# A mixture-of-experts stage that fetches its token tiles by lists: one-hot products in place of scattered rows, three routing groups, W2 split by GpSimd

## The reference, cut to what matters

```python
logits = einsum('bsd,de->bse', x, router_W) + router_b     # x: after a layernorm
probs = softmax(logits); top1 = argmax(probs)              # 8 experts, one for each token
h = relu(einsum('bsd,edf->besf', x, W1) + b1)              # 256 -> 1024
y = einsum('besf,efd->besd', h, W2) + b2                   # 1024 -> 256
out = x_before_norm + one_hot(top1) * probs . y            # only the chosen expert counts
```

## Time and profile before

| | us |
|---|---|
| median of 3 timed runs (lowest, highest) | 2818.48 (2810.91, 2821.3) |
| the profiled execution | 2812.32 |
| its span, first to last instruction | 2810.5 |
| busy: PE, DVE | 2571.2, 1928.8 |
| busy: ACT, GpSimd | 1322.4, 1132.5 |
| the mixture in the span | from 2441.6 |

### The profile page before, as it was taken

The page is one execution under the profiler, slowest core; times in us unless marked ns, Lnnn a source line. Parts: engine busy times, 40 slices in busy tenths (PEclk is TensorE's granted clock), DMA queues, the critical chain, the costliest instruction groups (busy, mean ns, idle before and its releaser), DMA issues. The chain is left out here.

```text
span 2810.5 us, 50716 instructions
## 1 busy us (share of the span) xinstructions
PE 2571.2 (91%) x16973; PEld 1551.5 (55%) x16989; DVE 1928.8 (69%) x3654; ACT 1322.4 (47%) x2007; POOL 1132.5 (40%) x853
## 2 busy tenths in 40 slices
PE   7997899999967899999999999999889999749998
PEld 4775333333335556565656565656444444448997
DVE  5776798998778765657575756566477776665555
ACT  2433477666668643434343434333245554443333
POOL 3323433333047253535453535444454443152333
PEclk9999799999979999999999999999989999859999
DMA  5001322222111000000000000000133332246665
GB/s 171 0 0 40 78 66 62 64 72 59 32 60 46 1 2 2 1 1 1 2 1 1 1 2 1 2 1 1 52 83 86 77 84 71 55 155 229 218 214 194
DMA packets 105254, 160.71 MB, mean 57 GB/s; under 512 B 30877, under 2 KB 65704, under 8 KB 99432
## 3 DMA queue, kind: packets, MB, share of 16 engines
q1 hardware_dynamic: 100056, 148.01, 18.4%
q0 software_dynamic: 3408, 8.46, 0.8%
q10 hardware_dynamic: 1600, 1.61, 0.2%
HBM read 91.66 MB, written 14.96 MB: 38 GB/s over the span
## 5 line engine op out<-in xcount | busy, mean ns | idle before, releaser
L1647 ACT ACTIVATE self_PT<-self_ST 128x1024 f32<-128x1024 f32 x256 | 263.0, 1027 | 483.1 <-PE self_ST L1586 480.5
L1667 DVE TENSOR_REDUCE self_nmax<-self_SM 128x2 fp32r<-128x1024 f32 x256 | 313.1, 1223 | 199.1 <-PE self_SM L1569 198.5
L1735 POOL TENSOR_TENSOR self_U<-self_PT 128x1024 f32<-128x1024 f32 x64 | 153.1, 2392 | 498.5 <-ACT self_PT L1647 498.5
L496 DVE TENSOR_REDUCE cross_nmax<-cross_S 128x2 f32<-128x1024 f32 x256 | 307.5, 1219 | 47.0 <-PE cross_S L350 44.9
L1738 POOL TENSOR_TENSOR self_U<-self_U,self_PT 128x1024 f32<-128x1024 f32 x128 | 303.9, 2374 | 82.2 <-ACT self_PT L1647 80.0
L441 ACT ACTIVATE cross_PT<-cross_S 128x1024 f32<-128x1024 f32 x256 | 259.9, 1025 | 124.4 <-PE cross_S L361 124.0
L1596 PE MATMUL self_W<-self_PT,self_V 128*64 128x512 f32 x1024 | 233.8, 598 | 0.0
L1141 DVE TENSOR_REDUCE cross_nmax<-cross_S 128x4 f32<-128x1024 f32 x128 | 156.5, 1223 | 92.7 <-PE cross_S L968 91.6
L1078 ACT ACTIVATE cross_PT<-cross_S 128x1024 f32<-128x1024 f32 x128 | 131.1, 1024 | 128.0 <-PE cross_S L984 127.7
L1596 PEld LDWEIGHTS self_W<-self_PT,self_V 128*64 128x64 f32 x1024 | 67.8, 136 | 131.8 <-issue 115.6
L1569 PE MATMUL self_SM<-self_k_hi,self_q_hi 64*128 64x512 f32 x512 | 117.7, 456 | 22.9 <-DVE self_nmax L1667 20.1
(11 more groups left out here) (450 smaller groups left out, 6893.6 us busy)
## 6 DMA issues: line engine op xcount, KB each, us to landing
moe_staged<-in_L_ffn_W SPq DMA_DIRECT2D x36, 1024.0 KB
cross_ks<-cross_parts SPq DMA_DIRECT2D x384, 64.0 KB, 2.3
cross_qs<-cross_parts SPq DMA_DIRECT2D x376, 64.0 KB, 2.3
all_x<-in_L_ffn_W SPq DMA_DIRECT2D x14, 1024.0 KB
all_x<-sorted_rows SPq DMA_DIRECT2D x83, 130.0 KB, 2.2
cross_cT<-in_ctx_T SPq DMA_DIRECT2D x16, 512.0 KB, 4.6
sorted_rows<-all_spare_row SPq DMA_DIRECT2D x1, 5460.0 KB, 23.8
all_x<-in_x SPq DMA_DIRECT2D x8, 512.0 KB, 9.2
```

The costliest lines, as they stand in the source:

```text
L496: dve.tensor_reduce(nmax[:, g % 2, 0:R, n % PER_G], S[:, slot[st], :, :], AX.X, ALU.max, negate=True).then_inc(s_maxed, 1)
L1647: act.activation(PT[:, k, :, :], ST[:, :, :], ACT.Exp).then_inc(exped.sem, 1)
L1667: dve.tensor_reduce(nmax[:, i:2 * NT:NT], SM[:, :, :], AX.X, ALU.max, negate=True).then_inc(maxed.sem, 1)
L1735: pool.tensor_tensor(U[:, c % 2, :, :], PT[:, 0, :, :], PT[:, 1, :, :], ALU.add).then_inc(added.sem, 1)
```

## The change

Rows are no longer sorted in memory. x, with 1/std and -mean/std, is written as it stands to DRAM (`rows_mem`, 4097 rows of 258 words, the last one zeros), by four DMAs that ACT issues ahead of the normalisations of a stretch. For each routing group, now three of 12, 12 and 8 tiles, DVE splits each token's position into a tile and a lane (`spread`), and forms two one-hot arrays: lanes (tokens x 128) and slots (tokens x 42, once times the token's number less 4096, once times its gate). PE multiplies them (`invert`) and adds up over all tiles in one PSUM bank, so that column n holds the list of slot n: for each lane the token's number and its gate. DVE adds 4096 and copies the lists (`places`, `gates`); an empty lane gets number 4096, the row of zeros, and its output is dropped.

The product of a group stands in PE's order ahead of the logits of pair 11 (group 0), behind the last logits (group 1) and behind the last count (group 2). GpSimd gathers each slot's tile from `rows_mem` by an indirect DMA, two slots further ahead than SP did, and `rest` is a copy that ACT makes of xs (`keep`). In the loop SP is left with W1 alone. Experts 0 to 6 get their low part of W2 from GpSimd, behind its roots and ahead of the gathers; expert 7's is DVE's, behind the lists. ACT makes the high parts two pieces at a time at pairs 3 to 6, 9 to 12 and 15 (`PIECES`), 18 of 32, and the other 14 after the last exponentials. W1 of slot 0 waits for the owners and for the four writes of x. The filling of the 5.46 MB at the start is one row now.

```diff
-XROW = C + 4
-GATE, TOKEN, RSTD, SHIFT = C, C + 1, C + 2, C + 3
-GROUPS, NORMS = ((0, 4), (4, 12), (12, 22), (22, 32)), ((0, 4), (4, 12), (12, 22), (22, 32))
-
-
-SPLIT_FROM = 3
+XROW = C + 2
+RSTD, SHIFT = C, C + 1
+SPARE = B * T
+GROUPS, NORMS = ((0, 12), (12, 24), (24, 32)), ((0, 4), (4, 12), (12, 22), (22, 32))
+
+
+PIECES = (0, 0, 0, 2, 2, 2, 2, 0, 0, 2, 2, 2, 2, 0, 0, 2)
+LOWS_BY_DVE = (7,)
...
+    hot_lanes, hot_tiles = (m.hid_hi, m.hid_lo), s.sb("hot_tiles", [P, MOST, 2, N_SLOTS])
...
+    def low_part(eng, e):
+        eng.wait_ge(s_w2_hi, FF // 2 * (e + 1))
+        eng.tensor_tensor(m.W2[:, e, :, 1, :], m.staged[:, e % 2, :, :], m.W2[:, e, :, 0, :].bitcast(F32),
+                          ALU.subtract).then_inc(m.s_w2_low[e % 2], 1)
...
-                sp.wait_ge(m.s_w2_low, e - 1)
+                sp.wait_ge(m.s_w2_low[e % 2], e // 2)
             sp.dma_start(m.staged[:, e % 2, :, :], a["L1_ffn_W2"][e].rearrange("(k p) n -> p k n", p=P)).then_inc(s_w2[e % 2], 16)
-        sp.wait_ge(s_sc, 16 * NX)
...
-        def scatter(g):
-            first, last = GROUPS[g]
-            pool.wait_ge(s_pos, g + 1)
-            for t in range(first, last):
-                pool.indirect_dma_start(out=sorted_rows, out_offset=bass.IndirectOffsetOnAxis(ap=position[:, t:t + 1], axis=0),
-                                        in_=x_rows[:, t, :], in_offset=None).then_inc(s_sc, 16)
...
-        for g in range(G):
-            scatter(g)
+        for e in range(E):
+            if e not in LOWS_BY_DVE:
+                low_part(pool, e)
...
+        def spread(g):
+            first, last = GROUPS[g]
+            n = last - first
+
+            def per_slot(v):
+                return v[:, 0:n].unsqueeze(2).to_broadcast([P, n, N_SLOTS])
+
+            step(dve.tensor_scalar(tile_of[:, 0:n], row[:, 0:n], P / 2 - 0.5, 1.0 / P, ALU.subtract, ALU.mult))
+            step(dve.tensor_scalar(tile_of[:, 0:n], tile_of[:, 0:n], ROUND, None, ALU.add))
+            step(dve.tensor_scalar(tile_of[:, 0:n], tile_of[:, 0:n], ROUND, None, ALU.subtract))
+            step(dve.scalar_tensor_tensor(out=lane_of[:, 0:n], in0=tile_of[:, 0:n], scalar=-float(P), in1=row[:, 0:n], op0=ALU.mult, op1=ALU.add))
+            if g:
+                dve.wait_ge(s_inv, g)
+            for at, to in ((0, min(n, FF)), (FF, n)):
+                if at < to:
+                    step(dve.tensor_tensor(hot_lanes[at // FF][:, 0:to - at, :], lane.unsqueeze(1).to_broadcast([P, to - at, P]),
+                                           lane_of[:, at:to].unsqueeze(2).to_broadcast([P, to - at, P]), ALU.is_equal))
+            placed, gated = hot_tiles[:, 0:n, 0, :], hot_tiles[:, 0:n, 1, :]
+            step(dve.tensor_tensor(placed, slot_no.unsqueeze(1).to_broadcast([P, n, N_SLOTS]), per_slot(tile_of), ALU.is_equal))
+            step(dve.tensor_tensor(gated, placed, per_slot(gate), ALU.mult))
+            step(dve.tensor_tensor(placed, placed, token[:, first:last].unsqueeze(2).to_broadcast([P, n, N_SLOTS]), ALU.mult))
+            dve.sem_inc(s_spread, 1)
...
             place(g)
-            if g < G - 1:
-                low_parts(g)
+            spread(g)
...
+        dve.wait_ge(s_inv, G)
+        step(dve.tensor_scalar(taken[:, :], inverse[:, 0, :], float(SPARE), None, ALU.add))
+        step(dve.tensor_copy(m.places[:, :], taken[:, :]))
+        step(dve.tensor_copy(m.gates[:, :], inverse[:, 1, :]))
+        dve.sem_inc(m.s_places, 1)
+        for e in LOWS_BY_DVE:
+            low_part(dve, e)
...
+        def invert(g):
+            first, last = GROUPS[g]
+            pe.wait_ge(s_spread, g + 1)
+            for t in range(first, last):
+                of = lanes_of(t - first)
+                done = pe.matmul(INV[:, 0:2 * N_SLOTS], of.bitcast(F32), hot_tiles[:, t - first, :, :].rearrange("p v n -> p (v n)"),
+                                 start=(t == 0), stop=(t == NX - 1), skip_group_check=True)
+            done.then_inc(s_inv, 1)
...
-            if 2 * m - 2 in [first for first, _ in GROUPS[1:]]:
+            if 2 * m - 2 in firsts:
                 count_of(group_of(2 * m - 2) - 1)
+            if 2 * m - 10 in firsts:
+                invert(group_of(2 * m - 10) - 1)
             logits(m)
+        invert(G - 2)
         count_of(G - 1)
+        invert(G - 1)
...
+                        act.dma_start(rows_mem[first * P:last * P, :].rearrange("(n p) c -> p n c", p=P), x_rows[:, first:last, :]).then_inc(s_rows, 16)
...
-            if i >= SPLIT_FROM:
-                high_part(i - SPLIT_FROM)
+            for piece in range(sum(PIECES[0:i]), sum(PIECES[0:i + 1])):
+                high_part(piece)
...
+    def keep(act, j):
+        act.copy(rest[:, j, :], xs[:, j, 0:C]).then_inc(s_kept, 1)
+
+    def gather(pool, n):
+        pool.indirect_dma_start(out=xs[:, n % DEEP, :], out_offset=None, in_=consts["rows_mem"],
+                                in_offset=bass.IndirectOffsetOnAxis(ap=m.places[:, n:n + 1], axis=0)).then_inc(s_loaded[n % DEEP], 16)
...
+        sp.wait_ge(m.s_rows, 16 * len(NORMS))
         m.load_w1(sp, 0, expert_of(sp, 0))
+        sp.dma_start(b2B[:, :], a["L1_ffn_b2"].rearrange("e c -> (e c)").unsqueeze(0).partition_broadcast(P)).then_inc(s_b2, 16)
...
-                following, stored = sp.snap(t * DEEP + (j + DEEP)), sp.snap(t * DEEP + (j + DEEP - 1))
-                sp.wait_ge(s_normed, t * DEEP + (j + 1))
-                sp.dma_start(xs[:, j, :], tiles[bass.ds(following, 1), :, :].rearrange("a p c -> (a p) c")).then_inc(s_loaded[j], 16)
                 sp.wait_ge(s_first, t * DEEP + (j + 1))
                 m.load_w1(sp, j, expert_of(sp, t * DEEP + (j + DEEP)))
-                k = (j + DEEP - 1) % DEEP
-                sp.wait_ge(s_freed, t * DEEP + (j + DEEP))
-                sp.dma_start(rest[:, k, :], tiles[bass.ds(stored, 1), :, :].rearrange("a p c -> (a p) c")).then_inc(s_rest[k], 16)
...
                 high_by_act(act)
+                act.wait_ge(s_y, t * DEEP + (j + 1))
+                keep(act, (j + 2) % DEEP)
...
-                dve.wait_ge(s_rest[j], t * 16 + 16)
+                dve.wait_ge(s_kept, t * DEEP + (j + 1))
                 dve.wait_ge(s_freed, t * DEEP + (j + 1))
-                dve.scalar_tensor_tensor(out=y[:, j, :], in0=z[:, :], scalar=rest[:, j, GATE:GATE + 1], in1=rest[:, j, 0:C],
+                dve.scalar_tensor_tensor(out=y[:, j, :], in0=z[:, :], scalar=m.gates[:, bass.ds(t * DEEP + j, 1)], in1=rest[:, j, :],
...
+        pool.wait_ge(consts["filled"], 16)
+        pool.wait_ge(m.s_rows, 16 * len(NORMS))
+        pool.wait_ge(m.s_places, 1)
+        for n in range(DEEP):
+            gather(pool, n)
         pool.wait_ge(s_hi_act, 1)
         low_by_pool(pool)
+        for n in range(DEEP, DEEP + 2):
+            pool.wait_ge(s_kept, n - DEEP + 1)
+            gather(pool, n)
         for n in range(SLOTS):
             pool.wait_ge(s_hi_act, n + 2)
             low_by_pool(pool)
+            if n + DEEP + 2 < SLOTS + AHEAD:
+                pool.wait_ge(s_kept, n + DEEP)
+                gather(pool, n + DEEP + 2)
             pool.wait_ge(s_y, n + 2)
...
         def fill(sp):
-            sp.wait_ge(s_id2, 2)
-            sp.wait_ge(s_spare, 16)
-            sp.dma_start(sorted_rows.rearrange("(g p) c -> p g c", p=P),
-                         spare_row[:, :].unsqueeze(1).to_broadcast([P, SLOTS + AHEAD, XROW])).then_inc(s_filled, 16)
+            sp.wait_ge(s_id2, 1)
+            sp.dma_start(rows_mem[SPARE:SPARE + 1, :], spare_row[:, :]).then_inc(s_filled, 16)
```

More of the change, by code:

```diff
@@ L2665 @@
 AHEAD, DEEP = 3, 3
-XROW = C + 4
-GATE, TOKEN, RSTD, SHIFT = C, C + 1, C + 2, C + 3
-GROUPS, NORMS = ((0, 4), (4, 12), (12, 22), (22, 32)), ((0, 4), (4, 12), (12, 22), (22, 32))
-SPLIT_FROM = 3
+XROW = C + 2
[4 more added lines that the diff above has]
+LOWS_BY_DVE = (7,)
 class MoeBuffers:
     def __init__(self, s, x_all, a):
-        self.s_w2_low, self.s_owned, self.s_b1 = s.sem("w2_low"), s.sem("owned"), s.sem("b1_in")
+        self.s_w2_low, self.s_owned, self.s_b1 = [s.sem(f"w2_low{n}") for n in range(2)], s.sem("owned"), s.sem("b1_in")
+        self.s_places, self.s_rows = s.sem("places"), s.sem("rows")
         self.s_w1 = [s.sem(f"w1_in{n}") for n in range(DEEP)]
@@ L2773, in route, with lanes_of @@
     s_w2, s_w2_hi = [s.sem(f"w2_in{n}") for n in range(2)], s.sem("w2_hi")
-    s_d, s_less, s_exp, s_hot, s_cnt, s_pos, s_sc = (s.sem(n) for n in ("d", "less", "exp", "hot", "cnt", "pos", "sc"))
+    s_d, s_less, s_exp, s_hot, s_cnt, s_pos = (s.sem(n) for n in ("d", "less", "exp", "hot", "cnt", "pos"))
+    s_spread, s_inv, s_rows = s.sem("spread"), s.sem("inv"), m.s_rows
+    def low_part(eng, e):
+        eng.wait_ge(s_w2_hi, FF // 2 * (e + 1))
+        eng.tensor_tensor(m.W2[:, e, :, 1, :], m.staged[:, e % 2, :, :], m.W2[:, e, :, 0, :].bitcast(F32),
+                          ALU.subtract).then_inc(m.s_w2_low[e % 2], 1)
+    def lanes_of(t):
```

(22 more changed lines are left out.)

70 lines of the change are left out of this document (28 added, 42 removed).

## The result

The changed kernel takes 2831.7 us (median of 5 runs, 2828.33 to 2833.5), against 2813.21 for the kernel before in the same comparison (5 runs, 2810.91 to 2821.3): a ratio of 1.0053, 95% interval 1.0036 to 1.007. By the ratio it is slower by about 15 us (the two medians are 18.5 us apart), just beyond the 0.5% that was set as the edge of no change; the interval reaches to both sides of that edge. The forecast was 2825, with 2803 to 2838 around it and most of the chance (0.65) within 0.5%. The profiled execution took 2830.98 us, its span is 2829.2.

What follows compares the result with a forecast made beforehand. PE bounds the loop, and a chain through 32 scatters the routing's end. Routing +10.5 and start -1.0 sum to +9.5 on the profiled 2812.32, so 2821.8; 2825 us was forecast for the measured median, range 2803 to 2838.

Steps and rivals of the forecast that it cites:

- The holds: In routing, GpSimd's low parts block DVE's steps with two SBUF operands: 4.7, 9.1 and about 9.5 us on the path.
- The owners: End of routing on DVE: the owners' table, 2.9 us of work with three groups, ready at 2538.3.
- the lists: End of routing: slot lists there at 2539.7, after 3.4 us for invert 2 from 2535.5.
- Invert 0: PE's product for group 0, ahead of pair 11 and so on the path: 5.2 us for 12 tiles.
- a low part: GpSimd's 128x2048 subtraction for an expert's W2 in routing: 4.55 us, bounds 4.3 and 5.0.
- The first rival: In routing, low parts run beside DVE or fall into its waits for PE: 2804 us; chance 0.20.
- The first gather: Between lists and first product: 2.9 us from issue to landing, then 1.7 for norm, turn and copy.
- The start: PE's first projection, behind a barrier after the filling, begins at 17.0 through the one-row filling: -1.0 us, or 0.
- The loop: The 39 slots, with fewer SP DMAs and an added gather and copy: cost 0, bounds 0 and +0.3 a slot.
- the second rival: The loop leaves PE because the gather delays DVE's last step: 39 x 0.3 = 12 us, together 2837; chance 0.15.
- the choice of +10.5: Delay of the first product taken as 2542.9, between sums of 2544.4 (12.0 late) and 2541.
- The third rival: In routing, half of the holds fall into waits: first product 2532 to 2538, time 2815 to 2819; chance 0.15.

Runs made afterwards that it cites:

- e2: The changed kernel with GpSimd filling the low parts of experts 0 to 6 with zeros, not subtracting two arrays; 2812.91 us, ratio 0.998 to the kernel before.
- e6: The changed kernel with invert 0 ahead of pair 12 of the logits, not pair 11; 2833.33 us, one run.
- e7: The changed kernel with GpSimd's low part of expert 2 waiting for spread 0; 2823.59 us, ratio 1.0027 to the kernel before.
- e5: The changed kernel with DVE's low part of expert 7 waiting for GpSimd's mark behind the first three gathers; 2832.28 us, one run.
- e4: The changed kernel with SP asking for W1 of slots 1 and 2 only once the first gather has landed; 2829.72 us, one run.
- e12: e10_mixed with SP asking for the 1 MB of b2 only once the first gather has landed; 2812.8 us, ratio 0.9985 to the kernel before.
- e10_mixed: The changed kernel with low parts shared by GpSimd (four pieces each) and DVE, invert 0 and high parts reordered; 2816.76 us, ratio 1.0003 to the kernel before.
- e9: The changed kernel with each of GpSimd's low parts as four instructions of 128x512, not one of 128x2048; 2832.24 us, one run.
- e3: The changed kernel with all eight low parts made by DVE; 2838.23 us, ratio 1.0075 to the kernel before.
- e8: The changed kernel with all low parts by DVE, groups of 8, 12 and 12 tiles, high parts and loads reordered; 2817.82 us, ratio 1.0006 to the kernel before.

## Why the prediction was right, and where its terms were off

**The holds** were the point, and right: 24.0 us measured, where the sum had 4.7 + 9.1 + 9.5 = 23.3. The owners were forecast at 2538.3 and ready at 2539.4 in a mixture that began 1.06 us later; the lists at 2539.7 and at 2540.9. Invert 0 took 5.41 (5.2 forecast), a low part 4.51 (4.55). That the owners agree so closely is in part luck. In group 2 the sum had 9.5 us of holds and 2.9 of waiting for invert 1; measured were 11.4 of holds and no such wait, since a held step covered it. In group 0 the holds came to 12.6, where the sum had 13.8, and `choose` and `place` took 9.6 by themselves, where it had 8.7. e2 shows that the holds cost 20.5 us of the owners' time (there DVE does wait for PE's count behind invert 1, 2.53 us, most of the difference from 24.0), e6 that invert 0 is on the path, and e7 that a hold counts only where DVE has no wait to lay it in. The first rival had the low parts beside DVE at 2804; with their reads taken away (e2) the time is 2812.91, since the first gather is late there too (7.53 us from issue to landing) and the owners are ready 76.2 us after the mixture's start, where that rival's sum had 74.0.

**The first gather was mis-sized**, the largest error of the sum. From the lists to the first product I had 2.9 + 1.7 = 4.6 us; it was 10.44: 1.0 until GpSimd's issue, which I had not counted, 7.61 to the landing and 1.83 behind it. The 2.9 came from the output's scatter in the loop, where no loads had just been asked for. The trace of before had shown how a scatter beside DVE's L2905 lasts 3.05, and 7.60 for the last scatters' landing; I used neither for this transfer. The error is 5.8 us. With low 7 moved off the issue, and W1 of slot 2 with it, the landing came 1.3 us sooner (e5), with W1 of slots 1 and 2 held back as much (e4), and with b2 held back in the mixed version 2.7 (e12). These overlap: all of them gone took 3.75 (7.61 in the changed kernel, 3.86 in e12).

**The start gained 0.14 us, not 1.0.** PE's first projection began 0.97 sooner, at 17.04, as forecast from the earlier trace rows, but its 24 calls took longer by 0.83:

```profile
17.04 13.08 PE L1990 MATMUL band_W<-band_hT,band_w 128*128 128x512 f32 x24 [5.41 <-PEq L1928]
21.44 0.34 PEld L1990 LDWEIGHTS band_W<-band_hT,band_w 128*128 128x128 f32 x1 [0.52 <-issue]
22.23 0.19 PEld L1990 LDWEIGHTS band_W<-band_hT,band_w 128*128 128x128 f32 x1 [0.45 <-issue]
```

The first calls of this run follow each other at 0.86 us, the others at 0.43, and their weight loads take 0.34 us and then 0.19. Before there were four slow calls, here nearly six, in e10_mixed between three and four. This is the pace of the two levels of TensorE's clock: at a granted clock of 0.50 (1.2 GHz) the weight loads of the router logits take 0.33, at 1.00 (2.4 GHz) those of the loop 0.19. A window of these microseconds shows 1.00, but no record stands behind it: the trace's first record of the granted clock begins at 22.15 us, in the kernel before at 21.47 and in e10_mixed at 20.39, and the pace doubles just there. Before it PE had been idle for 5.41 us, and then made the slow calls. So these ran most likely at the lower level, and the clock rose 0.68 us later here although PE began 0.97 sooner; what set the time of the rise is not shown. Whether the 1.06 us by which the mixture began later has to do with it is open, since the thirteen profiles differ by 10.

**The loop** cost nothing, and the second rival falls: 277.9 us from the first product to the end, before 278.1. DVE's last step of a slot (L3209 in the earlier trace rows, 486 to 1512 ns) is still held, for a shorter time than most were and alike in all slots. The source line, and one slot in the timelines of GpSimd and DVE:

```profile
L3251 DVE SCALAR_TENSOR_TENSOR all_x<-all_x,moe_gates x39: 757/773/776, 2567.5 to 2818.5; 128x256 f32<-128x256 f32 x39
...
2705.13 1.55 POOL L3107 TENSOR_TENSOR moe_hid_lo<-all_x,moe_hid_hi 128x512 fp32r<-128x512 f32 x1 [2.60 <-ACT moe_hid_hi L3101]
2706.18 0.77 DVE L3251 SCALAR_TENSOR_TENSOR all_x<-all_x,moe_gates 128x256 f32<-128x256 f32 x1
2706.82 0.99 POOL L3126 DMA_INDIRECT all_x<-rows_mem,moe_places  x1
```

In all 39 slots it begins inside GpSimd's low part and ends 0.28 us behind it. The gather, issued right behind the low part, doesn't keep it from its turn, which is what the second rival feared, and PE stays busy for 50.00 of 50 us.

**The time.** By the ratio the kernel lies 0.03% outside the 0.5% in which the forecast had put 0.65 of the chance, in the 0.26 of slower; the interval allows both. The profiled execution came out 9.2 above the forecast of 2821.8: the gather 5.8, the choice of +10.5 where the sum gave 12.0 (1.5), and the later mixture with the lost gain at the start (2.1). The third rival, half of the holds in waits, had the first product 90.4 to 96.4 us after the mixture's start; it came after 108.6, and with one more wait (e7), which lays two holds into a wait, after 101.7.

## What to carry to other kernels

Before giving an idle GpSimd an instruction that reads two arrays, ask what DVE does in those microseconds: small two-operand steps on the path each wait for the whole of it. Put such work where DVE waits for another engine, or cut it into short instructions, and count one piece for each DVE step, not the sum of the pieces. And a transfer that ends a chain should be priced from a row with the same traffic around it: here the first gather took 7.61 or 3.86 us, by the loads asked for around it and the instruction of DVE beside its issue.

## What was not expected of the hardware

- A fill of 128x2048 by GpSimd (1.80 us), which writes but reads nothing, held no step of DVE (e2). The Trainium skill ("SBUF — State Buffer", section "Who interferes with whom") says so of instructions that only write; the trace agrees.
- One-operand steps can be held too: a tensor_scalar on 128x8 lasted 3.97 us beside a low part where it takes 0.17, while reductions and steps with an operand in PSUM went on. The same section of the Trainium skill counts tensor_scalar among the operations that can take the shared ports; the trace agrees for this one.
- The waiting engine gets the next turn: in e9, with pieces of 128x512, DVE's steps in a row each waited for one piece, three beside the low part of expert 2 (1.72, 1.63, 1.63 us, alone 0.68) and three beside that of expert 5 (1.20, 1.18, 1.25, alone 0.17 to 0.23).
- The first indirect DMA of the gathers lasted 1.23 us on GpSimd with nothing beside it, the next ones 0.95; where DVE had begun an instruction with two SBUF operands (128x2048, 2.29 us) before it, 1.62 to 3.19. Such an issue ended a fixed time behind that instruction of DVE: the first gather's 1.1 us behind it (changed kernel, e3, e8), the second's 0.8 (e3, e5, e8). Its length on GpSimd said little of its landing: 3.19 with 5.02, 2.55 with 7.61.
